# Expert phase of a gated cross-attention block: the loads of rows move from SyncE's queue to ScalarE's

## The chip, the cores and the metric

The kernel runs on one core of one Trainium2 chip. The metric is the device time of one execution in microseconds (us); the median of several runs counts. Engines are called as the profile calls them: PE (TensorE), DVE (VectorE), ACT (ScalarE), POOL (GpSimd) and SP (SyncE). A name with a q behind it (ACTq, SPq) is the engine's sequencer, the part that reads the instructions, works on registers, waits and issues DMAs.

## The reference

Two layers, each with cross-attention and a feed-forward part, work on x of shape 32 x 112 x 256. The last part, a mixture of 64 experts, is the one that the change touches:

```
aff = xf @ centroids.T;  _, idx = top_k(aff + expert_biases, 8)
w = sigmoid(take_along_axis(aff, idx, 1));  w = w / (sum(w) + 1e-8)
cw = zeros((T, E)).at[arange(T)[:, None], idx].add(w)
h = silu(einsum('td,edf->etf', xf, W_up))
y = einsum('etf,efd->etd', h, W_down)
routed = einsum('etd,te->td', y, cw)
x = x + tanh(g_ffn[1]) * (shared + routed)
```

There are T = 3584 tokens of D = 256 numbers, E = 64 experts with F = 128 hidden numbers, and each token goes to 8 experts.

## The kernel before

Layer 0 and layer 1 run image by image. While layer 1 runs, POOL scatters a row for each token and each of its 8 experts into a table in DRAM, `expert_rows`, sorted by expert; a row is the 256 numbers, the place where its result belongs, and its weight. Both weight tensors of all experts lie in SBUF (`wup`, `wdn`) when the last phase begins, and so does a table (`table`, in a piece of `wq`) with two numbers for each tile: its expert and its first row.

The last phase, `expert_phase`, is the subject. It works on N = 288 tiles of 128 rows. Each engine runs a program of its own, written out by hand, and semaphores join them. What a tile n goes through:

- SP, `load` (L2030 to L2033): waits until the results of tiles up to n - 8 are made (`res_made`), reads the tile's first row from the table into a register (`from_table`, L2023, a TENSOR_LOAD), and issues the DMA of 129 KB from `expert_rows` into `xr`, a ring of RB = 8.
- PE, `turn_rows` (L2065): transposes the tile, two matmuls of 128 x 128. DVE, `keep_xT` (L2121, L2122): computes the destinations and copies the transposed tile to SBUF.
- ACT, `stage_weights` (L2151): reads the tile's expert from the table (L2023) and copies the expert's up-weights to a ring of 4. PE, `up` (L2073): the first product.
- ACT, `silu` (L2156). PE, `down` (L2081): the second product, on `wdn` at the expert's place.
- ACT, `keep_result` (L2162): waits for `res_out`, that the scatter from the same of 8 buffers has landed, and for PE, then writes `res` times the row's weight.
- POOL (L2053): an indirect DMA that scatters `res` into `expert_results`.

On ACT, body n does `stage_weights(n + 3)`, `keep_result(n - 1)` and `silu(n + 1)`, in this order. Bodies 0 to 15 are written out, then a loop of 16 rounds with 16 bodies each follows, then bodies 272 to 287 are written out. In the loop, indices depend on a register and cost register operations (FUSED_REGOPS in the trace, ISA in a listing of the order).

When the scatters are done, SP loads `expert_results` in 28 pieces, DVE adds the 8 results of each token to the residual `x3`, and ACT stores the output (L2182, L2186). SP loads the residual into `x3` in 7 DMAs of 512 KB: it issues each right behind one of the loads of tiles 9 to 15 (L2039).

Of the kernel before, what the change touches and what calls it, by code (L numbers as in the profile page):

```python
# [13 lines left out]
P = 128  # L14
# [31 lines left out]
def wait(eng, sem, value):  # L46

    if isinstance(value, int) and value <= 0:
        return
    eng.wait_ge(sem, value)  # L50
# [110 lines left out]
def experts_shape(t):  # L161

    NB, NQ, _ = t["x"].shape
    E = t["L1_ffn_W_up"].shape[0]
    cap = -(-NB * NQ // P) * P + P
    tiles = (TOP_K * NB * NQ + (P - 1) * E) // P
    return cap, -(-tiles // 16) * 16


def allocate(nc, es, t):  # L170

    def sb(name, shape):
        return es.enter_context(nc.sbuf_tensor(name, shape, F32))
# [4 lines left out]
    E = t["L1_ffn_W_up"].shape[0]  # L178
    CC = D // P
    w = dict(  # L180
# [4 lines left out]
        cf=sb("cf", [P, D]),  # L185
        cenT=sb("cenT", [P, CC, E]),
        ebias=sb("ebias", [P, E]),
        wq1=sb("wq1", [P, CC, INNER]), wk1=sb("wk1", [P, INNER]),
        wv1=sb("wv1", [P, INNER]),
# [4 lines left out]
        chosen=sb("chosen", [NQ, E]),  # L194
        sup=sb("sup", [P, CC, P]), sdn=sb("sdn", [P, D]),
    )
# [3 lines left out]
def allocate_a(nc, es, t):  # L200

    def sb(name, shape):
        return es.enter_context(nc.sbuf_tensor(name, shape, F32))

    NB, NQ, D = t["x"].shape
    CC = D // P
    w = dict(
        wq0=sb("wq0", [P, CC, D]), wk0=sb("wk0", [P, D]), wv0=sb("wv0", [P, D]),
        wo0=sb("wo0", [P, CC, D]),
# [1741 lines left out]
def expert_phase(nc, t, w, bank, rows_d, results_d, x3_d, out, table, beyond, wup, wdn):  # L1951
# [8 lines left out]
    E = t["L1_ffn_W_up"].shape[0]  # L1960
    CAP, N = experts_shape(t)
    RB = 8
    TURN = 16
    RES = 8
    DEST = 16
    HID, STAGE, DOWN = 4, 4, 4
    CC = D // P
    with ExitStack() as es:
        def sem(name):
            return es.enter_context(nc.semaphore(name))  # L1970

        def sb(name, shape):
            return es.enter_context(nc.sbuf_tensor(name, shape, F32))

        xr = sb("xr", [P, RB, D + 2])
# [3 lines left out]
        x_in = [sem(f"rows_in{b}") for b in range(RB)]  # L1979
        res_out = [sem(f"results_out{b}") for b in range(RES)]  # L1980
        x_turned, xT_out, upped, silued = sem("x_turned"), sem("xT_out"), sem("upped"), sem("silued")
        w_staged, downed, res_made = sem("w_staged"), sem("downed"), sem("res_made")
# [3 lines left out]
        OWN = NB * NQ // P  # L1986
        RUN, GAP = 4 * D, 8
        GROUP = RUN // D
# [5 lines left out]
        x3 = sb("x3_in", [P, OWN // GROUP, RUN + GAP])  # L1994
        x3_here, written = sem("x3_here"), sem("written")
# [4 lines left out]
        x3_rows = x3_d.rearrange(groups).rearrange("(p g r) -> p g r", p=P, r=RUN)  # L2000
        out_rows = out.rearrange(groups).rearrange("(p g r) -> p g r", p=P, r=RUN)

        def tiles(body):

            def f(eng):
                for b in range(TURN):
                    body(b, b)
                with eng.Fori(1, N // TURN - 1) as m:
                    for b in range(TURN):
                        body(m * TURN + b, b)  # L2010
                for b in range(TURN):
                    body(N - TURN + b, b)
            return f

        def inside(n):
            return not isinstance(n, int) or 0 <= n < N

        def passes(n, b, ring):

            return (n - b % ring) * (16 // ring)  # L2020

        def from_table(engine, n, column, most):
            return nc.values_load(table[0:1, bass.ds(n * 2 + column, 1)], engines=(engine,), min_val=0, max_val=most,  # L2023
                                  skip_runtime_bounds_check_because="the table is made with a minimum against this bound")

        with nc.Block() as block:

            @block.sync
            def _(sp):
                def load(n, b):  # L2030
                    wait(sp, res_made, n - RB + 1)
                    row = from_table(mybir.EngineType.SP, n, 1, E * CAP)
                    sp.dma_start(xr[:, b % RB, :], rows_d[bass.ds(row, P), :]).then_inc(x_in[b % RB], 16)  # L2033

                for b in range(TURN):
                    load(b, b)
                    g = b - (TURN - OWN // GROUP)
                    if g >= 0:
                        sp.dma_start(x3[:, g, :RUN], x3_rows[:, g]).then_inc(x3_here, 16)  # L2039
                with nc.sync.Fori(1, N // TURN) as m:  # L2040
                    for b in range(TURN):
                        load(m * TURN + b, b)
                for b in range(RES):
                    sp.wait_ge(res_out[b], 16 * (N // RES))
                for n in range(OWN):
                    wait(sp, added, n - GOT + 1)
                    sp.dma_start(got[n % GOT][:, :, :RUN], results[:, n]).then_inc(arrived[n % GOT], 16)
# [97 lines left out]
            @block.scalar  # L2145
            def _(act):
                def stage_weights(n, b):

                    wait(act, upped, n + 1 - STAGE)
                    e = from_table(mybir.EngineType.Activation, n, 0, E - 1)  # L2150
                    nc.scalar.copy(staged_w[:, b % STAGE, :], wup[:, bass.ds(e, 1), :].rearrange("p o d -> p (o d)")).then_inc(w_staged, 1)  # L2151

                def silu(n, b):

                    act.wait_ge(upped, n + 1)
                    nc.scalar.activation(hidT[:, b % HID, :], bank[2 + b % 2][:, :P], ACT.Silu).then_inc(silued, 1)  # L2156

                def keep_result(n, b):

                    wait(act, res_out[b % RES], passes(n, b, RES))  # L2160
                    act.wait_ge(downed, n + 1)
                    nc.scalar.activation(res[:, b % RES, :], bank[4 + b % DOWN][:, :D], ACT.Copy, scale=xr[:, b % RB, D + 1:D + 2]).then_inc(res_made, 1)  # L2162

                for n in range(3):
                    stage_weights(n, n)
                silu(0, 0)

                def body(n, b):
                    if inside(n + 3):
                        stage_weights(n + 3, (b + 3) % RB)  # L2170
                    if inside(n - 1):
                        keep_result(n - 1, (b - 1) % RB)
                    if inside(n + 1):
                        silu(n + 1, (b + 1) % RB)

                tiles(body)(nc.scalar)
                keep_result(N - 1, RB - 1)
                half = GROUP // 2
                for g in range(OWN // GROUP):
                    if g < OWN // GROUP - 1:  # L2180
                        act.wait_ge(added, (g + 1) * GROUP)
                        act.dma_start(out_rows[:, g], x3[:, g, :RUN]).then_inc(written, 16)  # L2182
                    else:
                        for a in range(2):
                            act.wait_ge(added, g * GROUP + (a + 1) * half)
                            act.dma_start(out_rows[:, g, a * half * D:(a + 1) * half * D],  # L2186
                                          x3[:, g, a * half * D:(a + 1) * half * D]).then_inc(written, 16)
                act.wait_ge(written, 16 * (OWN // GROUP + 1))
# [57 lines left out]
```

## Time and profile before

| | |
|---|---|
| median of 3 runs | 2541.04 us (2540.92 to 2542.85) |
| the profiled execution's own time | 2540.87 us |
| its span in the trace | 2539.1 us |
| busy: PE, DVE, ACT, POOL | 92%, 64%, 63%, 29% of the span |
| mean granted PE clock | 0.971 |
| expert phase: first tile's load to last scatter's issue | about 2071 to 2451 us |
| the sums and stores behind it | about 2451 to 2539 us |

Times in the trace count from the start of the span. The span is 1.8 us shorter than the execution's own time, which lies around it. Busy shares are means over phases that differ; the phase at hand covers 15% of the span.

### The profile page before, as it was taken

The page shows a single profiled execution, that of the slowest core. Times are in us where ns is not written, and L with a number is a line of the kernel's source. Part 1 is how long each engine was busy: PE and PEld are TensorE (multiplying, and loading weights), DVE is VectorE, ACT ScalarE, POOL GpSimd, SP SyncE. Part 2 cuts the span into 40 slices and gives each one's busy share as a digit, 9 for nine tenths or more (in the row PEclk, how much of TensorE's full clock was granted, in tenths as well). Part 3 has the DMA queues.
Part 4 walks back from the last instruction along what each step waited for, and adds up shares of the span by engine and source line. Part 5 has one row for each costly group of instructions (what it writes and reads, how often), then busy time and mean ns, then how long its engine had stood idle before and what let it go on. Part 6 is the DMA issues. An engine that isn't in the chain of part 4 may idle for free. (4 is left out here: it accounts for less than half of the span.)

```text
span 2539.1 us, 63423 instructions
## 1 busy us (share of the span) xinstructions
PE 2343.4 (92%) x19770; PEld 1769.9 (70%) x19771; DVE 1622.2 (64%) x5039; ACT 1607.2 (63%) x4900; POOL 729.3 (29%) x863
## 2 busy tenths in 40 slices
PE   7999999999998999999999999999999969999940
PEld 5777777777776566666666666666666658888830
DVE  4776776776774467677677667767767644333349
ACT  3777777777774566666666656656666527777730
POOL 2000000000000013323323323323322347777740
PEclk8999999999999999999999999999999979999975
DMA  5111111111112311111111111111111276666659
GB/s 156 42 39 46 49 36 46 49 36 49 46 32 62 110 30 42 41 36 42 44 34 47 41 31 47 42 33 44 42 37 37 68 237 203 192 194 196 193 180 380
DMA packets 145290, 210.06 MB, mean 83 GB/s; under 512 B 23977, under 2 KB 108507, under 8 KB 145027
## 3 DMA queue, kind: packets, MB, share of 16 engines
q1 hardware_dynamic: 114322, 139.92, 18.5%
q0 software_dynamic: 26544, 60.21, 7.0%
q10 hardware_dynamic: 4160, 6.55, 0.7%
q8 instruction: 150, 2.46, 0.4%
q14 instruction: 114, 0.93, 0.1%
HBM read 118.21 MB, written 96.75 MB: 85 GB/s over the span
## 5 line engine op out<-in xcount | busy, mean ns | idle before, releaser
L1454 ACT ACTIVATE wup<-bank,nmax 112x375 f32<-112x375 f32 x512 | 296.7, 585 | 111.8 <-DVE nmax L1558 110.6
L766 ACT ACTIVATE prob<-bank,nmax 112x375 f32<-112x375 f32 x512 | 293.8, 587 | 55.5 <-DVE nmax L850 51.5
L850 DVE TENSOR_REDUCE nmax<-bank 112x1 f32<-112x375 f32 x512 | 254.6, 539 | 90.3 <-PE bank L588 90.3
L2053 POOL DMA_INDIRECT expert_results<-res,dest x288 | 280.2, 973 | 105.6 <-issue 63.5
L1901 POOL DMA_INDIRECT expert_rows<-rows,ids x248 | 237.2, 956 | 154.3 <-ACT wup L1454 107.3
L1558 DVE TENSOR_REDUCE nmax<-bank 112x1 f32<-112x375 f32 x512 | 255.2, 540 | 20.6 <-PE bank L1250 20.6
L1313 PE MATMUL bank<-wup,wk 128*128 128x375 f32 x512 | 219.9, 512 | 2.0 <-DMA wup<-context_turned 0.8
L1019 POOL TENSOR_TENSOR stats<-stats,neg_half 112x1 f32<-112x1 f32 x64 | 35.1, 548 | 633.3 <-DVE stats L880 629.4
L1460 ACT COPY pT<-bank 128x336 f32<-128x336 f32 x512 | 201.4, 451 | 18.5 <-PE bank L1257 18.2
L1250 PE MATMUL bank<-wup 64*112 64x375 f32 x1024 | 195.3, 499 | 3.3 <-ACT wup L1454 3.3
L1868 POOL TENSOR_TENSOR stats<-stats,neg_half 112x1 f32<-112x1 f32 x64 | 35.6, 557 | 564.9 <-DVE stats L1589 562.6
L595 PE MATMUL bank<-ident,prob 112*128 112x112 f32 x1536 | 193.1, 261 | 4.3 <-ACT pT L772 2.3
L2081 PE MATMUL bank<-wdn,wo 128*128 x576 | 187.6, 408 | 8.8 <-ACT wo L2156 5.8
L2121 DVE TENSOR_TENSOR dest<-xr,wq 128x1 uint32<-128x1 f32 x288 | 46.4, 161 | 233.2 <-PE bank L2065 231.0
L1322 PE MATMUL bank<-wv,wup 128*128 128x512 f32 (+1 forms) x384 | 191.8, 608 | 1.0 <-ACT wup L1482 0.7
L1257 PEld LDWEIGHTS bank<-ident,wup 112*128 112x128 f32 x1536 | 163.1, 141 | 38.4 <-issue 26.7
L1257 PE MATMUL bank<-ident,wup 112*128 112x112 f32 x1536 | 189.3, 259 | 0.3 <-ACT pT L1460 0.3
L2073 PEld LDWEIGHTS bank<-wo 128*128 128x128 f32 x1152 | 174.5, 192 | 15.0
L2162 ACT ACTIVATE res<-bank,xr 128x256 f32<-128x256 f32 x288 | 136.3, 473 | 74.2 <-DMA expert_results<-res,dest 61.3
L1283 PEld LDWEIGHTS bank<-pT,wup 128*64 128x64 f32 (+1 forms) x3072 | 148.6, 136 | 43.5 <-issue 33.3
L1283 PE MATMUL bank<-pT,wup 128*64 128x112 f32 (+1 forms) x3072 | 176.2, 263 | 1.9 <-DVE x L1733 1.4
L595 PEld LDWEIGHTS bank<-ident,prob 112*128 112x128 f32 x1536 | 162.6, 142 | 21.1 <-issue 9.6
(254 smaller groups left out, 5035.5 us busy)
## 6 DMA issues: line engine op xcount, KB each, us to landing
xr<-expert_rows SPq DMA_DIRECT2D x288, 129.0 KB
wup<-expert_results SPq DMA_DIRECT2D x14, 1024.0 KB, 18.4
wdn<-expert_results SPq DMA_DIRECT2D x14, 1024.0 KB, 20.3
wdn<-in_L_ffn_W_down_dram SPq DMA_DIRECT2D x8, 1024.0 KB, 12.5
expert_rows<-nowhere SPq DMA_DIRECT2D x56, 129.0 KB, 2.9
x_and_h_in<-stage SPq DMA_DIRECT2D x32, 224.0 KB, 2.4
xt<-x_and_h_in SPq DMA_DIRECT2D x32, 224.0 KB, 2.8
context_turned<-ctxT SPq DMA_DIRECT2D x32, 187.5 KB, 2.1
```

What stands on the lines that cost most here:

```text
L595: mm = pe.transpose(pt_bank[n % 2][:, c * NQ:(c + 1) * NQ], prob[:, n % RING, c * P:(c + 1) * P], ident[:NQ, :NQ])
L766: nc.scalar.activation(prob[:, n % RING, :NK], s_bank[r][:NQ, :NK], ACT.Exp, bias=nmax[:, r:r + 1], accum_out=rsum[:, par, h:h + 1]).then_ ...
L850: nc.vector.tensor_reduce(nmax[:, r:r + 1], s_bank[r][:NQ, :NK], AX, ALU.max, negate=True).then_inc(maxed, 1)
L1250: pe.matmul(s_bank[r][:NQ, :NK], qT[par][rows_of, p, :], kT[par][rows_of, p, :], start=True, stop=True).then_inc(scored, 1)
L1257: mm = pe.transpose(pt_bank[n % 2][:, c * NQ:(c + 1) * NQ], prob[:, n % RING, c * P:(c + 1) * P], ident[:NQ, :NQ])
L1283: mm = pe.matmul(out[DK * b:DK * b + DK, a * NQ:(a + 1) * NQ], vals[:size, c, DK * m:DK * m + DK], pT[:size, m % PT_RING, c * NQ:(c + 1) * ...
L1313: mm = pe.matmul(misc[:, :NK], w["wk1"][:, p * P:(p + 1) * P], ctxT[par][:], start=True, stop=True)
L1454: nc.scalar.activation(prob[:, n % RING, :NK], s_bank[r][:NQ, :NK], ACT.Exp, bias=nmax[:, r:r + 1], accum_out=rsum[:, par, n:n + 1]).then_ ...
L1460: nc.scalar.copy(pT[:, n % PT_RING, :], pt_bank[n % 2][:, :KC * NQ]).then_inc(kept_act, 1)
L1558: nc.vector.tensor_reduce(nmax[:, r:r + 1], s_bank[r][:NQ, :NK], AX, ALU.max, negate=True).then_inc(maxed, 1)
L1901: nc.gpsimd.indirect_dma_start(rows_d, bass.IndirectOffsetOnAxis(ap=ids[:, k:k + 1], axis=0), rows[:, k, :], None).then_inc(scattered, 16)
L2053: nc.gpsimd.indirect_dma_start(results_d, bass.IndirectOffsetOnAxis(ap=dest[:, n % DEST:n % DEST + 1], axis=0), res[:, n % RES, :], None, ...
```

## The change

After the change SP issues the loads of the first six tiles and then, at once, the 7 loads of the residual. The loads of tiles 6 to 287 are issued by ACT: body n issues that of tile n + 6, between `stage_weights(n + 3)` and `keep_result(n - 1)`. It waits on the same condition as before (the results of tiles up to n - 2 are made), takes the row from the table by a TENSOR_LOAD of its own, and issues the DMA. The loads' sizes, the rings and the other engines' programs stay as they are.

```diff
+    AHEAD = RB - 2
...
             def _(sp):
-                def load(n, b):
-                    wait(sp, res_made, n - RB + 1)
+                for n in range(AHEAD):
                     row = from_table(mybir.EngineType.SP, n, 1, E * CAP)
-                    sp.dma_start(xr[:, b % RB, :], rows_d[bass.ds(row, P), :]).then_inc(x_in[b % RB], 16)
-
-                for b in range(TURN):
-                    load(b, b)
-                    g = b - (TURN - OWN // GROUP)
-                    if g >= 0:
-                        sp.dma_start(x3[:, g, :RUN], x3_rows[:, g]).then_inc(x3_here, 16)
-                with nc.sync.Fori(1, N // TURN) as m:
-                    for b in range(TURN):
-                        load(m * TURN + b, b)
+                    sp.dma_start(xr[:, n, :], rows_d[bass.ds(row, P), :]).then_inc(x_in[n], 16)
+                for g in range(OWN // GROUP):
+                    sp.dma_start(x3[:, g, :RUN], x3_rows[:, g]).then_inc(x3_here, 16)
...
+                def load(n, b):
+
+                    wait(act, res_made, n - RB + 1)
+                    row = from_table(mybir.EngineType.Activation, n, 1, E * CAP)
+                    act.dma_start(xr[:, b, :], rows_d[bass.ds(row, P), :]).then_inc(x_in[b], 16)
+
...
                 def body(n, b):
                     if inside(n + 3):
                         stage_weights(n + 3, (b + 3) % RB)
+                    if inside(n + AHEAD):
+                        load(n + AHEAD, (b + AHEAD) % RB)
                     if inside(n - 1):
                         keep_result(n - 1, (b - 1) % RB)
```

This is ACT's program before, inside the loop of the expert phase, one tile from the register work of `stage_weights` to the next `silu`; wq is where the table lies, wo where the staged weights and the hidden tile lie:

```order
L2023 ISA
L2023 TENSOR_LOAD wq
L2151 ISA
L2151 COPY wo<-wup 128x256
L2162 ACTIVATE res<-bank,xr 128x256
L2156 ACTIVATE wo<-bank 128x128
```

This is the same place on ACT after the change (the lines' numbers are lower by 7 there, and `from_table` is L2024):

```order
L2024 ISA
L2024 TENSOR_LOAD wq
L2144 ISA
L2144 COPY wo<-wup 128x256
L2024 ISA
L2024 TENSOR_LOAD wq
L2161 ISA
L2161 DMA xr<-expert_rows 128x258
L2155 ACTIVATE res<-bank,xr 128x256
L2149 ACTIVATE wo<-bank 128x128
```

Four rows have come in between the copy of the weights and the writing of the result, in every tile of the loop: register work, a second table read, register work and the DMA. In the bodies that are written out the two `L2024 ISA` are missing.

This is SP's program before, at the loads of tiles 9 and 10, where loads of the residual (x_in) stand between loads of rows:

```order
L2023 TENSOR_LOAD wq
L2033 ISA
L2033 DMA xr<-expert_rows 128x258
L2039 DMA x_in<-x 128x1024
L2023 TENSOR_LOAD wq
```

And this is SP's program after the change, from the load of the sixth tile on:

```order
L2024 TENSOR_LOAD wq
L2033 ISA
L2033 DMA xr<-expert_rows 128x258
L2035 DMA x_in<-x 128x1024 x7
L2040 DMA wup<-expert_results 128x2x1024 x7
```

The residual now follows the sixth tile's load in one piece, with no load of rows behind it on this queue, and the loads of the results are next.

## Rows read from the trace of the kernel before

**Rows 1.** Window 2105:2440, PE alone: busy, granted clock, DMA share, GB/s.

```profile
2105.00:2440.00 335.00, 324.26 (x2134) 1.00 0.63 187
```

**Rows 2.** Timeline of POOL: start, us, line, operation, idle time before and its releaser.

```profile
2300.64 0.97 POOL L2053 DMA_INDIRECT expert_results<-res,dest  x1 [0.30 <-issue]
2301.92 0.97 POOL L2053 DMA_INDIRECT expert_results<-res,dest  x1 [0.31 <-issue]
...
2450.13 0.97 POOL L2053 DMA_INDIRECT expert_results<-res,dest  x1 [0.30 <-issue]
```

**Rows 3.** Waits of ACT, 2105 to 2440: us in total, times, longest.

```profile
ACT res L2162 <- DMA expert_results<-res,dest: 60.1, 144, 2.5
...
ACT res L2162 <- PE bank L2081: 4.3, 5, 1.2
```

**Rows 4.** Timeline of ACT inside the loop.

```profile
2304.66 0.47 ACT L2162 ACTIVATE res<-bank,xr 128x256 f32<-128x256 f32 x1 [0.59 <-DMA expert_results<-res,dest]
...
2305.22 0.40 ACT L2151 COPY wo<-wup 128x256 f32 x1
2305.62 0.47 ACT L2162 ACTIVATE res<-bank,xr 128x256 f32<-128x256 f32 x1
...
2306.15 0.40 ACT L2151 COPY wo<-wup 128x256 f32 x1
...
2308.33 0.47 ACT L2162 ACTIVATE res<-bank,xr 128x256 f32<-128x256 f32 x1 [0.50 <-DMA expert_results<-res,dest]
...
2309.04 0.41 ACT L2151 COPY wo<-wup 128x256 f32 x1
```

**Rows 5.** Line of the table reads: count, ns min/median/max, first and last start.

```profile
L2023 ACTq TENSOR_LOAD <-wq x288: 275/282/664, 2070.1 to 2436.3; - x144
```

**Rows 6.** Line of SP's loads of rows, 2072.5 to 2077, same columns.

```profile
L2033 SPq DMA_DIRECT2D xr<-expert_rows x6: 332/333/333, 2072.9 to 2076.9; - x6
```

**Rows 7.** One load of SP inside the loop, 2306.18 to 2307.2.

```profile
L2023 SPq FUSED_REGOPS  x1: 69/69/69, 2306.2 to 2306.2; - x1
...
L2033 SPq FUSED_REGOPS  x1: 37/37/37, 2306.6 to 2306.6; - x1
...
L2033 SPq DMA_DIRECT2D xr<-expert_rows x1: 333/333/333, 2306.8 to 2306.8; - x1
```

**Rows 8.** Lines of ACT's own DMAs, at the end and the start.

```profile
L2182 ACTq DMA_DIRECT2D out_dram<-x_in x6: 338/338/379, 2468.5 to 2525.4; - x6
...
L332 ACTq DMA_DIRECT2D nat<-in_L_ffn_wi_dram x1: 487/487/487, 1.3 to 1.3; - x1
```

**Rows 9.** Timeline of ACT, the first result.

```profile
2076.88 0.47 ACT L2162 ACTIVATE res<-bank,xr 128x256 f32<-128x256 f32 x1
```

**Rows 10.** Waits of POOL, 2087.5 to 2101.3: us in total, times, longest.

```profile
POOL expert_results L2053 <- ACT res L2162: 6.1, 4, 1.9
POOL expert_results L2053 <- issue: 1.3, 3, 0.7
```

**Rows 11.** Timeline of PE at full clock.

```profile
2102.27 0.38 PE L2065 MATMUL bank<-ident,xr 128*128 128x128 f32 x2
...
2103.37 0.38 PE L2065 MATMUL bank<-ident,xr 128*128 128x128 f32 x2
```

**Rows 12.** Timeline of PE some tiles earlier.

```profile
2088.78 0.44 PE L2065 MATMUL bank<-ident,xr 128*128 128x128 f32 x2 [0.89 <-DMA xr<-expert_rows]
...
2091.08 0.51 PE L2065 MATMUL bank<-ident,xr 128*128 128x128 f32 x2 [0.96 <-DMA xr<-expert_rows]
...
2093.15 0.63 PE L2065 MATMUL bank<-ident,xr 128*128 128x128 f32 x2
```

**Rows 13.** Window 2091.4:2094.6, columns as in Rows 1.

```profile
2091.40:2094.60 3.20, 3.20 (x13) 0.50 1.05 413
```

**Rows 14.** Timeline of ACT where a round of the loop ends and the next begins.

```profile
2318.47 0.47 ACT L2162 ACTIVATE res<-bank,xr 128x256 f32<-128x256 f32 x1 [0.42 <-DMA expert_results<-res,dest]
...
2319.36 0.41 ACT L2151 COPY wo<-wup 128x256 f32 x1 [0.26 <-PE bank L2073]
```

## The prediction

> **What bounds the kernel now.** The page comes first: the phase at hand is the only long stretch in which POOL's digit stands at 7, and PE's is 9 as well, so that either could set the pace. The window over the loop says 97% for PE [rows 1], but that share is of modelled ends and proves nothing by itself. The timeline of POOL decides: its indirect DMAs start 1.28 us apart, 0.97 us of work and 0.30 us before the next, whatever the others do, up to the last at 2450.13 [rows 2]. The waits of ACT say the same from the other side: it stands 60.1 us in 144 places for a scatter that has to free a buffer of `res`, and only 4.3 us for PE [rows 3]. The results are there before POOL asks for them. PE can do more too: at full clock its tiles follow each other 1.10 us apart [rows 11]. So POOL sets the pace, 1.28 us for each tile, and PE has 0.18 us of slack in each.
>
> ACT's own slack is what the change spends, and it must be read from its sequencer, not from its busy time. The window's busy share is no guide to it, since a table read and a DMA issue count as no work of the engine. From the start of a `keep_result` to the start of the next copy of weights pass 0.53 to 0.56 us in most tiles (2304.66 to 2305.22, 2305.62 to 2306.15) and 0.71 in one (2308.33 to 2309.04) [rows 4]: the `silu` behind the result is handed to the engine at once, but the table read is done by the sequencer itself, 0.28 us at the median and up to 0.66 [rows 5], and the copy can't be handed over before it. I take 0.56 as the mean, since some reads are long. Behind the copy the sequencer has nothing to do but to wait for the next result.
>
> **The change, part by part.** Into that place comes a load. What it costs a sequencer is seen on SP, which does nothing else. Six loads of the bodies that are written out start from 2072.9 to 2076.9, 0.80 us each [rows 6], with nothing to wait for. Inside the loop the register work for the index comes first, 0.07 us at 2306.2, the table read starts at 2306.3, the DMA at 2306.8 and takes 0.33 [rows 7]; that is 0.1 us more, 0.90 in all. ACT's price for a DMA is no guess: it issues its stores in 0.338 us each at the median [rows 8], as SP does its loads. From the end of the DMA to the start of the next `keep_result` I put 0.1 us, an estimate: the gaps between SP's rows are some 0.03 (0.80 less 0.27, 0.04, 0.33 and another short row leaves 0.13 for four), and here come two, a wait on a semaphore and the hand-over.
>
> The wait on `res_made` adds nothing: it asks for the result of the `keep_result` before, whose 0.47 us are over before the copy of weights has started at 0.56 [rows 4]. Nor do the landings: a load is issued as early as before, right behind the same result, and PE asks for its rows four tiles later. What is queued behind the load on ACT is `keep_result(n - 1)`, for which POOL waits, then `silu(n + 1)`, for which PE waits, and these two move by the load's whole price.
>
> So a tile of the loop takes ACT 0.56 + 0.90 + 0.10 = **1.56 us**, against POOL's 1.28. The cover of 0.72 us (1.28 - 0.56) is smaller than the load's 1.0, and ACT becomes the pace of the phase. In the bodies written out there are no index computations, 0.1 us each in two places, 1.36, and I take 1.40 for long table reads. A round's end costs more: from the result to the copy pass 0.89 us there (2318.47 to 2319.36) [rows 14], of which 0.26 are a wait for PE at the end of it that would be gone or not; I put 0.45 for a round with the register work that follows it, a choice between 0.1 and 0.6.
>
> The sum, from the first result to the last scatter's issue:
> - the first result is made at 2076.88 [rows 9]; two loads now stand ahead of it, partly in time in which ACT waited for PE: 2078.4
> - 15 tiles of 1.40: 21.0
> - 256 tiles of 1.56: 399.4
> - 17 ends of rounds of 0.45: 7.7
> - 10 tiles of 1.40 that still load, and 6 without a load at 1.15 (PE's 1.10 and a little for waits): 20.9
> - the last result and its scatter, 0.47 + 0.05 + 0.97: 1.5
>
> That ends at 2528.9. Before, it was 2450.13 + 0.97 = 2451.1 [rows 2]. The difference is 77.8 us. What follows (the last scatters' landing, the sums, the stores) starts later and is not changed. On the execution's own 2540.87 us that makes 2618.7, and the median of the runs shown lies 0.2 us from it, so **2618 us**.
>
> SP's part costs nothing: its 288 loads hid behind POOL's pace, and 282 of them vanish. The residual's 3.5 MB now go out at 2076 to 2080 in one piece, beside the loads of tiles 6 to 10 and no longer ahead of them in the same queue. Before, POOL stood 7.4 us in seven gaps in the stretch where they were mixed [rows 10], 2.1 of which are its usual 0.30, so 5.3 us were lost. With ACT as the pace that place gives nothing back, as the 15 tiles of 1.40 are already slower than POOL.
>
> The bounds of a tile: the lowest is that the gaps I have read on SP overlap on ACT with the hand-overs, five of 0.03, so 1.41, and the time is 272 x 0.15 = 41 us less, 2577. The highest is that ACT's DMAs cost what they did at the kernel's start, 0.487 [rows 8], 0.15 more, and 282 x 0.15 = 42 us more, 2660.
>
> The Trainium skill (DMA: Bandwidth & Descriptors, section "Latency and other measured facts") gives a floor of some 600 ns for a `tensor_load`. By that figure a tile of the loop would hold two such reads and take about 0.6 us more, and the kernel would end near 2790 us, an estimate by that page. The trace does not agree: its reads take 275 ns at the least and 282 at the median [rows 5], and the measurement decides.
>
> **The rivals.**
>
> A. The load is covered and POOL stays the pace. What speaks for it: the rows alone, with no gap between them, are 0.28 and 0.06 for the weights and 0.07, 0.28, 0.04 and 0.34 for the load, 1.07 us and less than 1.28, and ACT idles 60.1 us for scatters [rows 3]. Against it: SP's loads, with nothing to wait for, never came closer than 0.80 us [rows 6]. It decides at a tile under 1.28 us. The time would be 2541, within 5 us.
>
> The Trainium skill (DMA: Bandwidth & Descriptors, section "Issuing engines are not separate DMA queues") says that the sequencer's time to start a DMA is usually small beside the DMA. By that rule the case is this one. No row shows the two side by side, but 0.33 us of issue is a quarter of a tile here, and it is the sequencer that is short.
>
> B. Faster: A holds, and the residual is out of the way of the rows. The one place is 2087.5 to 2101.3, the price the 5.3 us of POOL [rows 10], if rows of tiles 6 to 14 land in time. The time is 2535.6, just beyond 0.2%. It decides by the same 1.28 us.
>
> C. Slower still, by PE's clock. In the stretch where tiles came 2.2 to 2.3 us apart at PE (2088.78 to 2091.08) the granted clock fell to 0.50, which is 1.2 of 2.4 GHz, and a tile then took 2.07 us (2091.08 to 2093.15) [rows 12, 13]. At 1.28 us a tile the clock stayed at 1.00 [rows 1]. A distance of 1.56 lies between the two and nearer the latter. Were the clock half for half of the time, 272 tiles would cost 0.5 x 0.51 = 0.26 us more, 70 us: 2688.
>
> D. ACT's load is cheaper than any bound above, but over 1.28: a tile of 1.30 to 1.40, 2546 to 2575.
>
> E. It is dearer, by longer table reads or a DMA issue beyond 0.49: above 2660.
>
> **How the numbers follow.** The main case, ACT as the pace at 1.41 to 1.71 us a tile, has 0.70 and its own range is 2577 to 2660. A has 0.05, B 0.04, C 0.06, D 0.10, E 0.05. To leave out no more than 2 in 10 the range takes in the upper part of D and the near part of C and E: 2560 to 2675. A measurement of this kernel can tell about 0.2%, 5 us, from no change. Faster by more than that is B, 0.04; the same is A, 0.05; slower is the rest, 0.91.
>
> **What the profile of the changed kernel would show.** Right: POOL waits for ACT's result before nearly every scatter in the loop, and its starts are 1.5 to 1.6 us apart; ACT no longer waits for scatters; from a `keep_result` to the next copy still pass 0.53 to 0.56, and from the copy to the next result 0.9 to 1.05; ACT's DMAs of rows take 0.33 to 0.34 us; PE's waits in the loop turn to `silu` on ACT with the clock at 1.00; the stretch behind the last scatter is as long as before, 88 us. Wrong: POOL's starts stay 1.28 us apart (A, B), the clock falls in the loop (C), or ACT's DMAs take far from 0.33 (E). A starved PE, waiting for rows in the loop, would say that I was wrong on the landings.

## The result and the profile after

| | |
|---|---|
| median of 4 runs after | 2627.82 us (2627.14 to 2627.98) |
| median of 4 runs before | 2541.70 us (2540.92 to 2542.85) |
| ratio | 1.0338, 95% interval 1.0325 to 1.0350 |
| the profiled execution's own time, and its span | 2627.14 us, 2625.4 us |

The change costs 3.4%, 86 us. The forecast was 2618 us, and 2577 to 2660 for its main case.

First the timeline of POOL in the changed kernel, inside the loop and at the last scatter (start, us, line and operation, idle time before and its releaser), which answers to [rows 2]:

```profile
2313.65 0.97 POOL L2046 DMA_INDIRECT expert_results<-res,dest  x1 [0.68 <-issue]
2315.19 0.97 POOL L2046 DMA_INDIRECT expert_results<-res,dest  x1 [0.57 <-issue]
2316.72 0.97 POOL L2046 DMA_INDIRECT expert_results<-res,dest  x1 [0.56 <-issue]
...
2536.37 0.97 POOL L2046 DMA_INDIRECT expert_results<-res,dest  x1 [0.30 <-issue]
```

The scatters start 1.54 us apart instead of 1.28, and the last one ends at 2537.34 instead of 2451.10. These 86.2 us are the difference of the two executions (2627.14 - 2540.87 = 86.3). What stands behind is as long as before, 88 us.

Does POOL wait for ACT's result now? This is the line of POOL's scatters, 2312.5 to 2315.3:

```profile
L2046 POOLq MOVE  x2: 29/29/29, 2312.9 to 2314.4; - x2
```

The second of these moves starts at 2314.4, when the result begun at 2313.94 ends (2314.41), and the scatter that it belongs to starts at 2315.19. POOL's sequencer waits for the result and then needs some 0.74 us until the scatter starts. Of 263 such moves between 2105 and 2525, 260 start 0.03 us behind a result's end. So the scatters follow ACT's results, though the timeline calls the 0.57 us ahead of it "issue".

The timeline of ACT at the same place; rows with ACTq are DMA issues, and table reads are not shown in this view:

```profile
2312.40 0.47 ACT L2155 ACTIVATE res<-bank,xr 128x256 f32<-128x256 f32 x1 [0.70 <-PE bank L2074]
2312.78 0.27 ACT L2149 ACTIVATE wo<-bank 128x128 f32<-128x128 f32 x1
2312.94 0.40 ACT L2144 COPY wo<-wup 128x256 f32 x1
2313.50 0.34 ACTq L2161 DMA_DIRECT2D xr<-expert_rows  x1
2313.94 0.47 ACT L2155 ACTIVATE res<-bank,xr 128x256 f32<-128x256 f32 x1 [0.60 <-PE bank L2074]
```

From result to copy pass 0.54 us, as in [rows 4]. From the copy to the DMA's start pass 0.56, the DMA takes 0.34, and the next result starts 0.10 behind it. The wait for a scatter that stood at ACT before [rows 3] is gone. In its place the view names TensorE's second product. These are the waits of 2105 to 2525, ACT's, PE's and POOL's:

```profile
ACT res L2155 <- PE bank L2074: 151.6, 241, 1.0
...
PE bank L2074 <- ACT wo L2149: 55.2, 218, 0.9
...
POOL expert_results L2046 <- issue: 124.8, 226, 0.9
POOL expert_results L2046 <- ACT res L2155: 41.1, 38, 3.4
```

ACT seems to wait for PE 241 times, and PE for ACT's `silu` 218 times. The view puts ACT's idle time down to the semaphore that came last, and doesn't count that ACT's sequencer was busy all the while. The chain of work, 2311 to 2317, goes through the sequencer in some tiles and through PE in others:

```profile
2311.38 0.03 issue
2311.41 0.39 ACTq L2024
2311.80 0.03 issue
2311.83 0.04 ACTq L2161
2311.87 0.03 issue
2311.90 0.03 ACTq L2161
2311.93 0.03 issue
2311.96 0.34 ACTq L2161
2312.30 0.04 issue
2312.34 0.02 ACTq L2154
...
2312.81 0.24 ACT wo L2149
2313.05 0.13 issue
2313.18 0.71 PE bank L2074 x2
```

The first part is table read, register work, a move, the DMA and a wait, with 0.03 us between one and the next, as SP's rows had it. The second part says that the result at 2313.94 waited for the second product that ended at 2313.89, which in turn had waited for `silu`. Were that so, the pace would be a ring of ACT and PE and not the sequencer. But the order of the programs speaks against it. Behind `silu` of a tile ACT writes the result of the tile before that one, and the product for it is one earlier on PE's timeline:

```profile
2311.53 0.69 PE L2074 MATMUL bank<-wdn,wo 128*128 x2 [0.46 <-ACT wo L2149]
```

It ended at 2312.22, 1.7 us before the result started, and in 254 tiles of the loop, all but the first and the last, the product ended at least 1.59 us before the result that needs it. The load's DMA ended 0.10 to 0.18 us before the result in every one of them. The view of waits and the chain both name a product that is needed only a tile later.

The line of the loads, and the branch at the end of each round on ACT:

```profile
L2161 ACTq DMA_DIRECT2D xr<-expert_rows x282: 339/339/917, 2074.1 to 2525.7; - x141
DMA to landing us min/median/max: 2.0/2.1/3.5
...
L2009 ACTq COMPARE_BRANCH  x16: 40/45/63, 2126.5 to 2512.0; - x16
```

The window over the loop, PE alone, columns as in [rows 1]:

```profile
2105.00:2525.00 420.00, 360.98 (x2102) 1.00 0.49 149
```

A DMA costs ACT 0.339 us, and it lands 2.1 us after its issue, long before PE needs it. PE's clock stays at 1.00, the upper level, in this stretch. From the first of the rounds' branches to the last pass 385.5 us for 15 rounds, 25.70 each: 16 tiles of 1.54 and 1.06 more.

At the start of the phase the residual now goes out in one piece. The timeline of ACT there:

```profile
2083.04 0.34 ACTq L2161 DMA_DIRECT2D xr<-expert_rows  x1
2086.65 0.47 ACT L2155 ACTIVATE res<-bank,xr 128x256 f32<-128x256 f32 x1 [3.67 <-PE bank L2074]
2087.50 0.28 ACT L2149 ACTIVATE wo<-bank 128x128 f32<-128x128 f32 x1 [0.38 <-PE bank L2066]
```

One result comes 4.8 us behind the one before it. PE's waits of 2071 to 2105 say for what:

```profile
PE bank L2058 <- DMA xr<-expert_rows: 5.7, 6, 2.9
```

Rows are late there, beside 3.5 MB of residual: from 2076.4 to 2087 the DMA share is 0.98 to 1.03, against 0.49 in the loop.

### The profile page after: what moved, and what is told of

Its sections match the earlier page's. It is cut to its first block and busy times, and to the rows that moved or that the text cites. A ratio compares the mean times of both kernels' runs of the same rounds, so it can differ in the third digit from the quotient of the medians.

```text
span 2625.4 us, 63270 instructions
## 1 busy us (share of the span) xinstructions
PE 2387.5 (91%) x19770; PEld 1773.6 (68%) x19771; DVE 1620.0 (62%) x5039; ACT 1606.7 (61%) x4900; POOL 728.9 (28%) x863
## 5 line engine op out<-in xcount | busy, mean ns | idle before, releaser
L2074 PE MATMUL bank<-wdn,wo 128*128 x576 | 199.2, 428 | 58.7 <-ACT wo L2149 55.8
```

What stands on the lines that cost most here:

```text
L2074: pe.matmul(bank[4 + b % DOWN][:, :D], hidT[:, b % HID, :], wdn[:, bass.ds(e, 1), :].rearrange("p o d -> p (o d)"), start=True, stop=True) ...
```

## The experiments

The theory after the result was that of the prediction: ACT's sequencer has become the pace, since its serial work for a tile exceeds POOL's 1.28 us. The rivals were that the loads come late or slow other transfers, that PE is what is waited for (as the view of waits says), that the place of the load ahead of `keep_result` hurts, and that the residual's new place has a share. Each ratio below is to runs of the kernel before that were made beside it.

**All loads back on SP, the residual still in one piece.**

```diff
                 for g in range(OWN // GROUP):
                     sp.dma_start(x3[:, g, :RUN], x3_rows[:, g]).then_inc(x3_here, 16)
+                def later(n, b):
+                    wait(sp, res_made, n - RB + 1)
+                    row = from_table(mybir.EngineType.SP, n, 1, E * CAP)
+                    sp.dma_start(xr[:, b % RB, :], rows_d[bass.ds(row, P), :]).then_inc(x_in[b % RB], 16)
+                for b in range(AHEAD, TURN):
+                    later(b, b)
+                with nc.sync.Fori(1, N // TURN) as m:
+                    for b in range(TURN):
+                        later(m * TURN + b, b)
...
-                    if inside(n + AHEAD):
-                        load(n + AHEAD, (b + AHEAD) % RB)
```

> SyncE issues all loads of rows again, but the residual's 7 loads stay in one piece behind the sixth tile's load, as in the changed kernel. Theory (ScalarE's sequencer became the pace): GpSimd paces again at 1.28 us a tile, 2541 us, within 6. Rival (the residual's new place has a share in the 86 us): well above, 2550 or more.

Measured: 2546.93 us, ratio to before 1.0019 (1.0009 to 1.0029). Nearly all of the 86 us is the loads' move to ACT. The residual's place costs 5 us here. PE in this kernel:

```profile
2091.88 0.47 PE L2069 MATMUL bank<-ident,xr 128*128 128x128 f32 x1 [10.49 <-DMA xr<-expert_rows]
```

It stands 10.49 us for one tile's rows, whose load SP issued at 2082.30, behind the 3.5 MB in its queue.

**A second table read on ACT, loads on SP.**

```diff
-                    e = from_table(mybir.EngineType.Activation, n, 0, E - 1)
+                    e = (from_table(mybir.EngineType.Activation, n, 0, E - 1) + from_table(mybir.EngineType.Activation, n, 0, E - 1)) // 2
```

> As the kernel with all loads on SyncE and the residual in one piece, but ScalarE reads the expert's number from the table twice for each tile and uses the mean of the two. Theory: a tile costs ScalarE 0.53 + 0.31 + 0.1 us, still below GpSimd's 1.28, so the time is that of the kernel without the second read, within 5 us, near 2541. Rival (each table read lies on the path, as the sequencer is waited for): 288 x 0.31, 89 us more, near 2630.

Measured: 2547.87 us, 1.0022 (1.0011 to 1.0033), the same as the run without the second read. A table read alone fits under POOL's pace.

**The load on ACT, but one table read less.**

```diff
-                    e = from_table(mybir.EngineType.Activation, n, 0, E - 1)
-                    nc.scalar.copy(staged_w[:, b % STAGE, :], wup[:, bass.ds(e, 1), :].rearrange("p o d -> p (o d)")).then_inc(w_staged, 1)
+                    nc.scalar.copy(staged_w[:, b % STAGE, :], wup[:, b:b + 1, :].rearrange("p o d -> p (o d)")).then_inc(w_staged, 1)
```

> The changed kernel, with the loads and their table reads on ScalarE, but the copy of the up-weights takes a fixed expert, so that its own register work and table read are gone (the expert's choice for the first product is left out). Theory: a tile costs ScalarE 1.54 - 0.48 = 1.06 us, below 1.28, GpSimd paces again, 2541 to 2548. Rival (loads issued from ScalarE's queue arrive late or slow the other transfers): stays above 2600.

Measured: 2598.14 us, 1.0224 (1.0203 to 1.0246). Here the theory failed: only 30 us of 86 came back. ACT's timeline in this kernel:

```profile
2305.10 0.47 ACT L2154 ACTIVATE res<-bank,xr 128x256 f32<-128x256 f32 x1 [0.55 <-PE bank L2074]
2305.47 0.27 ACT L2148 ACTIVATE wo<-bank 128x128 f32<-128x128 f32 x1
2305.63 0.40 ACT L2143 COPY wo<-wup 128x256 f32<-128x256 f32 x1
2306.13 0.34 ACTq L2160 DMA_DIRECT2D xr<-expert_rows  x1
2306.57 0.47 ACT L2154 ACTIVATE res<-bank,xr 128x256 f32<-128x256 f32 x1 [0.54 <-PE bank L2074]
```

A tile takes 1.48 us, though the sequencer has 0.48 us less to do. The same kernel's line of register and table work, 2305.08 to 2306.5:

```profile
L2024 ACTq FUSED_REGOPS  x1: 69/69/69, 2305.6 to 2305.6; - x1
L2024 ACTq TENSOR_LOAD <-wq x1: 274/274/274, 2305.7 to 2305.7; - x1
```

The load's first register work starts at 2305.6, when the result begun at 2305.10 ends (2305.57). Its wait on `res_made`, for the tile six ahead, asks for exactly the result that ACT has begun last. The sequencer stands until that is written, 0.50 us, and only then reads the table. So the body has two lower bounds for the load's start behind the result: 0.50 us by the wait on that result, and 0.56 by the copy's table read. The theory was amended by this: to take work away ahead of the wait gives only the difference of the two, 0.06 us a tile or 17 us in all. Most of the other 13 us came at the rounds' ends: a round took 23.98 us here, 0.30 more than its 16 tiles of 1.48, where the changed kernel had 1.06 more.

**The same with loads five ahead.** The wait then asks for the result before.

```diff
-    AHEAD = RB - 2
+    AHEAD = RB - 3
```

> The kernel with ScalarE's loads and a fixed expert for the copy of the up-weights, but loads five tiles ahead instead of six, so that a load waits for the result before the last and not for the one that ScalarE has just begun (the expert's choice for the first product is left out). Theory (that wait holds the sequencer 0.50 us, which is why one read less gave so little): a tile falls from 1.48 to about 1.05 us, GpSimd paces again, 2541 to 2550. Rival (something else holds ScalarE's queue, such as the DMA's issue beside the engine's work): stays near 2598.

Measured: 2545.12 us, 1.0013 (1.0004 to 1.0022). ACT in this kernel:

```profile
2305.02 0.48 ACT L2154 ACTIVATE res<-bank,xr 128x256 f32<-128x256 f32 x1 [0.19 <-issue]
2305.39 0.27 ACT L2148 ACTIVATE wo<-bank 128x128 f32<-128x128 f32 x1
2305.55 0.41 ACT L2143 COPY wo<-wup 128x256 f32<-128x256 f32 x1
2305.70 0.34 ACTq L2160 DMA_DIRECT2D xr<-expert_rows  x1
2306.14 0.47 ACT L2154 ACTIVATE res<-bank,xr 128x256 f32<-128x256 f32 x1 [0.19 <-issue]
```

The DMA now starts 0.68 us behind the result instead of 1.03, and the next result, where nothing else holds it, 1.12 behind the one before. That is under POOL's 1.28, and POOL paces again. All but five of the loads come from ACT's queue here too, and the time is that of the kernel with all of them on SP (2546.93), so the rival on transfers is out: from this queue they cost nothing as such. `silu` starts 0.37 us behind the result as in the changed kernel, and PE's products are the same, so a ring of ACT and PE can't have been the changed kernel's pace either.

**Five ahead alone, on the changed kernel** (the same one line).

> The changed kernel with loads five tiles ahead instead of six. Theory: with both table reads in the body the sequencer reaches the load's wait at 0.53 us or later, when the result is already there at 0.50, so the wait is no part of the 1.54 us: 2628, within 6. Rival (the wait on its own result is a part of the loss): 0.05 us or more a tile less, 2613 or below.

Measured: 2629.60 us, 1.0348 (1.0332 to 1.0364), the time of the changed kernel. With both reads in the body the wait is not what binds. Five ahead gains 53 us with one read less, and nothing with both.

**A third table read.**

```diff
-                    row = from_table(mybir.EngineType.Activation, n, 1, E * CAP)
+                    row = (from_table(mybir.EngineType.Activation, n, 1, E * CAP) + from_table(mybir.EngineType.Activation, n, 1, E * CAP)) // 2
```

> The changed kernel with one more table read in each load on ScalarE (the row is the mean of two reads of the same number). Theory: each read is 0.28 and a gap of 0.03, straight on the path: 282 x 0.31 = 87 us more, 2715, between 2705 and 2725. Rival (the profile's own words, ScalarE waits for TensorE's second product): little change, 2628 to 2640.

Measured: 2753.08 us, 1.0837 (1.0818 to 1.0857), 125 us above the changed kernel. PE as the pace is out, since its work is the same. The size is off by 38 us. The line of the loads' register work, and a piece of the chain, 2150.5 to 2155.5:

```profile
L2161 ACTq FUSED_REGOPS  x282: 89/93/104, 2075.1 to 2649.3; - x141
...
2151.39 0.52 ACTq L2024
...
2151.94 0.28 ACTq L2024
```

The register work takes 0.09 us instead of 0.04, for the mean, which I had not counted. From branch to branch a round takes 32.95 us against 25.70, so 0.45 for a tile against the expected 0.31 and these 0.05. The rest, 0.09 us a tile, lies in the table reads: the first of the load's two reads took over 0.35 us in 118 of 247 tiles of the loop, as the one of 0.52 us shown, and 0.38 in the mean, against 0.29 for the load's read in the changed kernel. Why these reads are longer is not known.

**The load last in the body, behind `silu`.**

```diff
-                    if inside(n + AHEAD):
-                        load(n + AHEAD, (b + AHEAD) % RB)
                     if inside(n - 1):
                         keep_result(n - 1, (b - 1) % RB)
                     if inside(n + 1):
                         silu(n + 1, (b + 1) % RB)
+                    if inside(n + AHEAD):
+                        load(n + AHEAD, (b + AHEAD) % RB)
```

> The changed kernel with the load at the body's end, behind silu, instead of ahead of keep_result. Theory (throughput of the sequencer): the same sum for each tile, 2628 within 6 us. Rival (latency: what hurts is that keep_result stands behind the load): clearly below, 2550 to 2600.

Measured: 2629.38 us, 1.0357 (1.0336 to 1.0377). The place in the body makes no difference; the sum does. The rival is not tested sharply by this, since in a loop the next tile's `keep_result` stands behind the load there too.

**Half of the loads on each engine.**

```diff
-                    if inside(n + AHEAD):
+                    if inside(n + AHEAD) and (b + AHEAD) % 2:
                         load(n + AHEAD, (b + AHEAD) % RB)
```

SP issues the even ones, from tile 6 on, with a loop as in the first experiment.

> ScalarE issues the loads of odd tiles and SyncE those of even ones. Theory: two tiles cost ScalarE 1.54 + 0.96 = 2.50 us against GpSimd's 2.56, so it is hidden but for the heads of the loop's rounds: 2541 to 2556. Rival (any load on ScalarE costs its share): half of the 86 us, 2585.

Measured: 2547.75 us, 1.0024 (1.0014 to 1.0033), no more than with all loads on SP and the residual in one piece. So the loss is no share for each load but what exceeds POOL's pace.

**Rounds of 32 bodies.**

```diff
-    TURN = 16
+    TURN = 32
```

> The changed kernel with rounds of 32 bodies on all engines: 32 bodies written out at each end and 7 rounds between, instead of 16 and 16. Theory: each round's head costs about 1.0 us more than a tile's pace, and 9 of 16 go (9 us); 32 more tiles run written out at 1.38 instead of 1.54 (5 us): 2614, between 2608 and 2620. Rival (the extra at a round's head is not the loop's): 2623.

Measured: 2635.35 us, 1.0374 (1.0353 to 1.0395), slower instead of 14 us faster. ACT at a round's end in this kernel:

```profile
2392.01 0.47 ACT L2155 ACTIVATE res<-bank,xr 128x256 f32<-128x256 f32 x1 [0.60 <-issue]
2392.38 0.27 ACT L2149 ACTIVATE wo<-bank 128x128 f32<-128x128 f32 x1
2395.36 0.40 ACT L2144 COPY wo<-wup 128x256 f32 x1 [2.71 <-issue]
```

From the result to the copy pass 3.35 us, against 0.93 in the changed kernel at such a place. Fewer ends of rounds, but each much dearer: behind each of the six branches back ACT's sequencer does nothing for 2.45 to 2.65 us, against some 0.2 in the changed kernel, and behind the seventh, where the loop is left, it goes on at once. The page counts the packets of a DMA queue that it calls "instruction" (packets, MB, share of the 16 engines), in the changed kernel and in this one:

```profile
q14 instruction: 114, 0.93, 0.1%
...
q14 instruction: 149, 1.22, 0.2%
```

In the 16-body loop, from 2127 to 2512, 3 packets came by this queue; in the 32-body loop, from 2178 to 2498, it was 34, and one of them started 0.95 to 1.14 us behind each branch back. So with the longer body instructions are fetched again in every round. That ACT's stall is the wait for them fits these times, but no run changed it.

**The residual late.** SP waits for 64 results ahead of the residual's loads, in the changed kernel.

```diff
+                sp.wait_ge(res_made, 4 * TURN)
                 for g in range(OWN // GROUP):
```

> The changed kernel, but SyncE issues the residual's loads only when 64 results are made. Theory: the stall at tiles 5 to 7, some 5.5 us against the pace, is gone: 2622. Rival (the stall is only the loads' start): 2628.

Measured: 2624.35 us, 1.0333 (1.0314 to 1.0351), not to be told from the changed kernel's 1.0338 (1.0325 to 1.0350), so neither theory nor rival is decided by the time. In the profile the loss moves: at 2184 ACT idles 2.13 us ahead of a result, where the residual is on its way. The 3.5 MB disturb the rows there too, inside the loop.

**All loads on SP, the residual last.** This one starts from the kernel before.

```diff
-                    g = b - (TURN - OWN // GROUP)
-                    if g >= 0:
-                        sp.dma_start(x3[:, g, :RUN], x3_rows[:, g]).then_inc(x3_here, 16)
                 with nc.sync.Fori(1, N // TURN) as m:
                     for b in range(TURN):
                         load(m * TURN + b, b)
+                for g in range(OWN // GROUP):
+                    sp.dma_start(x3[:, g, :RUN], x3_rows[:, g]).then_inc(x3_here, 16)
```

> The kernel before, all loads of rows on SyncE, with the residual's 7 loads behind the last load of rows instead of between those of tiles 9 to 15. Theory: the 5.3 us that GpSimd lost at the start of the phase come back, and nothing is lost at the end, where the transfers are few: 2536, between 2534 and 2538. Rival (seen in the run with the residual late: the loss only moves): 2541.

Measured: 2536.74 us, 0.9982 (0.9973 to 0.9991), 4.3 us under the kernel before and the fastest of all kernels here. Timeline of POOL in this kernel, at the place of [rows 10]:

```profile
2089.57 0.97 POOL L2052 DMA_INDIRECT expert_results<-res,dest  x1 [0.30 <-issue]
2090.85 0.97 POOL L2052 DMA_INDIRECT expert_results<-res,dest  x1 [0.30 <-issue]
```

Where POOL idled 7.4 us in seven gaps, each gap is now 0.30.

## Why the prediction was right, by its own steps

**What bounded the kernel**: right. POOL's 1.28 us was the pace, and every kernel that left ACT under it (all loads on SP, half, one read less with five ahead, and the second read) came within 0.3% of before.

**A tile of ACT, 0.56 + 0.90 + 0.10 = 1.56 us**: 1.54 in most tiles. The trace of the changed kernel has 0.54 to the copy, 0.90 to the DMA's end and 0.10 to the next result. The first two had been read from rows of the kernel before, the third was an estimate. This is the step on which the forecast stood, and the rows of SP were a good price for ACT.

**The wait on `res_made` adds nothing**: right for this kernel, as the run with five ahead shows, but by little: 0.50 against 0.56. I had seen that the result is written by then, not that the wait would be a bound of its own once the work ahead of it shrinks. The run with one read less showed it.

**The landings cost nothing**: right in the loop (2.1 us to land, no wait of PE for rows). At the start it was wrong, see below.

**The sum.** It put the end of the loop's last round at 2078.4 + 21.0 + 399.4 + 7.7 = 2506.5, and the branch there is at 2512.0, 5.5 us later. The first result came at 2076.37, 2.0 us earlier than I put it; 1.6 of these are luck, as in this execution the whole phase began 1.6 us earlier (ACT's first table read at 2068.5 instead of 2070.1). The 15 tiles after it and the step into the loop, to 2101.1, took 24.7 us instead of 21.0: the stall of 4.8 us behind the residual, which I had said gives nothing back, took 3.4 us more than a tile. The rounds took 25.70 us, where I had 16 x 1.56 + 0.45 = 25.41; the tile was priced 0.02 too high and the round's end 0.6 too low. Behind the loop 25.3 us passed instead of 22.4: the last six tiles without a load ran at PE's pace on ACT, as I had it, but the scatters behind them at POOL's 1.28, and I had forgotten that POOL paces again as soon as ACT doesn't, seven scatters at 1.28 in place of results at 0.7 to 1.1. Together 8.4 us of the 86.3 were missing.

**The residual's new place costs nothing**: the step that failed. It costs some 5 us with the loads on SP, and a stall of 4.8 us with them on ACT. That it shows so little in the sum is luck: the estimate of the first result was 2 us too late, for another reason. What it costs the changed kernel as a whole stays open, since the run with the residual late can't be told from it.

**The rivals.** A and B hang on a tile under 1.28, and it is 1.54. C fell by the clock of 1.00 in the loop. D wanted 1.30 to 1.40, and E a dearer DMA than 0.49. B's gain exists, 4 us, but with the loads on SP and the residual last.

**The signs.** All came as forecast, but one is not in the view where I had looked for it: POOL's wait for ACT's result is named at 38 scatters only, and the other 226 gaps are called "issue". That they too follow ACT's result is seen from POOL's sequencer.

The Trainium skill (Perfetto Trace Analysis, section "Sequencer Loop") says that the sequencer pushes an instruction for the engine into a queue and executes a control instruction itself. The trace agrees: the table read runs beside the result's 0.47 us, and no engine instruction behind it starts before it ends (0.54 from result to copy).

The Trainium skill (DMA: Bandwidth & Descriptors, section "Issuing engines are not separate DMA queues") calls the time to start a DMA usually small. Beside the 2.1 us to land, 0.339 us is small here too. Yet it counts against the pace of the engine that issues, together with the table read that gives the address, and here the two made ACT the pace.

## What to carry to other kernels

Before work is moved to another engine's queue, add up that engine's sequencer for one turn (table reads, register work, DMA issues, and 0.03 us between them), not its busy time, and set it against the pace of the engine that binds. A load that waits for a result of the engine that issues it holds that engine's queue until the result is written, so issue it one turn further away; this gained 53 us where the wait was the later bound, and nothing where it wasn't. And a transfer that nobody needs until the end belongs behind the last of those that are waited for, which was worth 4 us here.

## What the runs showed of the hardware that I had not expected

The branch back at the end of a round: ACT's sequencer stood some 0.2 us with 16 bodies, and 2.45 to 2.65 us with 32 bodies, each of the six times. Packets of instructions came in every round there and almost none with 16 bodies. That it is this loading that is waited for was not tried.

A table read of ACT took 0.28 us at the median in all of these kernels, but about 0.5 in many tiles of the kernel with a third read. What makes it so is open.

The view of waits named PE 241 times for idle time of ACT in which ACT's sequencer was at work, and the chain did so too in some tiles. Where the sequencer is the resource, the lines with a q have to be added up, and the semaphore that a view names has to be checked against the tile that the program waits for.
